# A recommender tower on one core: id comparisons without row sums, ids in three runs with gaps, fewer chunks on ScalarE

## The reference

```python
e = jnp.stack([tbl_0[ids[:, 0]], ..., tbl_25[ids[:, 25]]], axis=1)   # tables of 1000, 1250, 12500 or 125000 rows
combined = jnp.concatenate([dense_features[:, None, :], sparse_features], axis=1)
interactions = jnp.einsum('bnd,bmd->bnm', combined, combined)
interactions_flat = interactions[:, _TRIU_I, _TRIU_J]
z = jnp.concatenate([dense_features, interactions_flat], axis=1)
h = jnp.concatenate([z, r_dense_features], axis=1)
h = jnp.maximum(h @ W_top1 + b_top1, 0.0)      # (607, 512)
h = jnp.maximum(h @ W_top2 + b_top2, 0.0)      # (512, 256)
y = h @ W_top3                                 # (256, 1)
```

## Time and profile before

| | us |
|---|---|
| median of 3 runs | 109.49 |
| lowest and highest | 109.1, 110.28 |
| the profiled execution | 109.33 |
| its span in the profile | 107.4 |
| busy: TensorE, VectorE, ScalarE, GpSimd | 98.3, 86.0, 64.4, 64.5 |

### The profile page before, as it was taken

The page is one execution under the profiler, slowest core; times in us unless marked ns, Lnnn a source line. Parts: engine busy times, 40 slices in busy tenths (PEclk is TensorE's granted clock), DMA queues, the critical chain, the costliest instruction groups (busy, mean ns, idle before and its releaser), DMA issues.

```text
span 107.4 us, 3972 instructions
## 1 busy us (share of the span) xinstructions
PE 98.3 (92%) x1657; PEld 80.4 (75%) x1657; DVE 86.0 (80%) x255; ACT 64.4 (60%) x110; POOL 64.5 (60%) x68
## 2 busy tenths in 40 slices
PE   5969897997999899998999999999999997999991
PEld 2337576764766788877899887999798866998890
DVE  4799999999999999999999999999572436078121
ACT  5699989999999997809989474846300040001210
POOL 3577778777777778777777777777777700000000
PEclk9999999999999999999999999999999999999999
DMA  2999985747567847999782852112222110000000
GB/s 59 319 288 329 396 266 169 206 135 228 168 173 236 247 146 219 329 326 315 252 279 63 227 167 55 49 49 55 55 58 67 52 31 6 0 6 0 0 6 1
DMA packets 10575, 16.19 MB, mean 151 GB/s; under 512 B 2352, under 2 KB 6478, under 8 KB 10558
## 3 DMA queue, kind: packets, MB, share of 16 engines
q1 hardware_dynamic: 8398, 11.62, 34.0%
q0 software_dynamic: 2016, 4.13, 13.3%
q10 hardware_dynamic: 144, 0.19, 0.5%
HBM read 15.94 MB, written 0.00 MB: 148 GB/s over the span
## 4 chain that ended last, share of the span: by engine, by line
POOL 57%; issue 18%; PE 15%; DMA 6%; POOLq 1%; DVE 1%; DVEq 0%
POOL rows_sb L530 57%; PE h_ps L675 3%; DMA rows_sb<-in_tbl,ids_sb 3%; PE h_ps L650 3%; DMA ids_sb<-in_ids 2%; PE gram_ps L594 2%; PE h_ps L619 1%; PE turn_ps L650 1%; POOLq L293 1%; PE gram_ps L650 1%; PE turn_ps L619 1%; PE h_ps L658 1%; PE gram_ps L611 1%; PE turn_ps L594 1%; PE place_ps L611 0%
## 5 line engine op out<-in xcount | busy, mean ns | idle before, releaser
L530 POOL DMA_INDIRECT rows_sb<-in_tbl,ids_sb x63 | 63.6, 1009 | 20.9 <-issue 18.9
L571 PE MATMUL turn_ps<-onehot_sb,high_sb 128*128 128x512 f32 (+2 forms) x118 | 41.9, 367 | 3.5 <-DVE low_sb L807 1.4
L798 DVE TENSOR_SCALAR_CACHE_REDUCE onehot_sb<-lookup_ids_sb,first_sb 128x256 fp32r<-128x256 int16 (+2 forms) x79 | 43.6, 598 | 0.0
L572 PE MATMUL turn_ps<-onehot_sb,low_sb 128*128 128x512 f32 (+2 forms) x118 | 38.9, 342 | 0.0
L571 PEld LDWEIGHTS turn_ps<-onehot_sb,high_sb 128*128 128x128 f32 x118 | 22.2, 188 | 9.5 <-DVE low_sb L807 2.4
L572 PEld LDWEIGHTS turn_ps<-onehot_sb,low_sb 128*128 128x128 f32 x118 | 22.3, 189 | 1.6
L739 ACT ACTIVATE onehot_sb<-lookup_ids_sb,first_sb 128x512 fp32r<-128x512 int16 (+2 forms) x31 | 18.8, 621 | 2.3 <-PE turn_ps L572 2.2
L807 DVE TENSOR_TENSOR low_sb<-table_sb,high_sb 128x640 fp32r<-128x640 f32 (+1 forms) x26 | 19.4, 757 | 0.0
L729 ACT CAST high_sb<-table_sb 128x640 fp32r<-128x640 f32 (+1 forms) x26 | 17.0, 672 | 3.0 <-PE turn_ps L572 2.8
L594 PE MATMUL gram_ps<-feats 128*32 128x27 f32 x960 | 12.8, 196 | 1.1 <-DVE feats L701 0.4
L747 ACT ACTIVATE onehot_sb<-onehot_sb 128x768 fp32r<-128x768 f32 (+4 forms) x13 | 13.6, 1049 | 0.1
(11 more groups left out here) (53 smaller groups left out, 74.2 us busy)
## 6 DMA issues: line engine op xcount, KB each, us to landing
table_sb<-in_tbl SPq DMA_DIRECT2D x13, 256.0 KB, 3.5
table_sb<-in_tbl SPq DMA_DIRECT2D x7, 320.0 KB, 3.6
lookup_ids_sb<-in_lookup_ids SPq DMA_DIRECT2D x12, 128.0 KB, 2.4
table_sb<-in_tbl SPq DMA_DIRECT2D x6, 192.0 KB
rows_sb<-in_tbl,ids_sb POOLq DMA_INDIRECT x63, 3.3
w1p_sb<-in_w_pairs SPq DMA_DIRECT2D x1, 768.0 KB
w1d_sb<-in_w_dense SPq DMA_DIRECT2D x1, 512.0 KB, 6.3
w_sb<-in_w SPq DMA_DIRECT2D x1, 512.0 KB, 6.0
```

The lines of the kernel that those rows point to most:

```text
L530: pool.indirect_dma_start(out=rows_sb[:, GATHERS.index((tile, slot)), :], out_offset=None, in_=tables[f], in_offset=bass.IndirectOffsetOnAxis(
L571: nc.tensor.matmul(bank, high_sb[0:rows, u % 2, c, :], picked, start=c == 0, stop=False)
L572: nc.tensor.matmul(bank, low_sb[0:rows, u % 2, c, :], picked, start=False, stop=c == CHUNKS[u] - 1).then_inc(chunk_used, 1)
L798: nc.vector.tensor_scalar(onehots(u, [c])[:, 0, :], lookup_ids_at(u), row_ids_sb[:, row:row + 1], None, ALU.is_equal, ALU.add, accum_out=m ...
```

## The change

VectorE's comparison loses its second operation and its second output, and is a plain compare. The ids of a lookup, which lay in one run of 512, 384 or 256 numbers, now lie in three runs of 172, 128 or 86 with a gap of two numbers behind each, and are read as three runs; the one-hot chunk that is written is one run of 516, 384 or 258. TensorE multiplies the first 512, 384 or 256 columns of it, as before. ScalarE's distances read the three runs too.

`ACT_CHUNKS` gives ScalarE 30 chunks, where it had 33: 14 (15) in lookups 0 to 5, 7 (7) in 6 to 8, 9 (11) in 9 to 12. VectorE makes the other 88 (85). All four order tables are written anew.

```diff
+ID_RUNS = 3
+def id_columns(u):
+    return B - LOOKUP_FROM[u] * P
+def id_run(u):
+    return 2 * -(-id_columns(u) // (2 * ID_RUNS))
+ID_GAP = 2
+IDS_MAX = ID_RUNS * (id_run(0) + ID_GAP)
-ACT_CHUNKS = [2,3]*6+[3]
+ACT_CHUNKS = [3, 2, 2] * 4 + [2]
...
-    lookup 0 0:8; lookup 1 0:8; turn 0 0; lookup 2 0:7; turn 0 1; lookup 2 7; lookup 3 0:3; turn 0 2; lookup 3
+    lookup 0 0:8; lookup 1 0:4; turn 0 0; lookup 1 4:8; lookup 2 0:2; turn 0 1; lookup 2 2:8; lookup 3 0:5; turn
...
 SP_ORDER = """
-    ids; table 0; id; table 1; table 2; dn; w1d; table 3; table 4; table 5; table 6; mask; table 7; table 8;
-    table 9; w1p; table 10; sm; w2; table 11; table 12
+    ids; table 0; id; table 1; table 2; table 3; table 4; w1p; w2; table 5; dn; w1d; table 6; table 7; sm; table
+    8; mask; table 9; table 10; table 11; table 12
...
         def lookup_ids_at(u):
             ids_at = lookup_ids_sb[:, u % TABLE_BUFS, :] if u > 0 else first_ids_sb
-            return ids_at[:, LOOKUP_FROM[u] * P:B]
+            ids_at = ids_at[:, 0:ID_RUNS * (id_run(u) + ID_GAP)].rearrange("p (r c) -> p r c", r=ID_RUNS)
+            return ids_at[:, :, 0:id_run(u)]
+        def onehot_runs(u, c):
+            return onehots(u, [c])[:, 0, :].rearrange("p (r c) -> p r c", r=ID_RUNS)
...
-                picked = onehots(u, [c])[0:rows, 0, :]
+                picked = onehots(u, [c])[0:rows, 0, 0:id_columns(u)]
...
-                nc.scalar.activation(onehots(u, [c])[:, 0, :], lookup_ids_at(u),
+                nc.scalar.activation(onehot_runs(u, c), lookup_ids_at(u),
                                      ACT.Abs, bias=row_ids_sb[:, row:row + 1], scale=-1.0).then_inc(distance_made, 1)
...
-                nc.vector.tensor_scalar(onehots(u, [c])[:, 0, :], lookup_ids_at(u),
-                                        row_ids_sb[:, row:row + 1], None, ALU.is_equal, ALU.add,
-                                        accum_out=matches_sb[:, row:row + 1]).then_inc(onehot_dve, 1)
+                nc.vector.tensor_scalar(onehot_runs(u, c), lookup_ids_at(u), row_ids_sb[:, row:row + 1], None,
+                                        ALU.is_equal).then_inc(onehot_dve, 1)
```

More of the change, by code:

```diff
@@ L235 @@
+    3 1 2; layer2 2 1; dense1 3 2 3; place 3 0 16; place 3 16 32; dense1 3 3 4; bias2 3; layer1 3 0 1; layer1 3
+    1 2; layer1 3 2 3; layer1 3 3 4; layer2 3 0; layer2 3 1
 """
 ACT_ORDER = """
-    distance 0 6; cast 0 0; distance 0 7; cast 0 1; distance 1 5; cast 1 0; distance 1 6; onehot 0; distance 1
-    7; onehot 1; cast 1 1; cast 2 0; distance 2 6; copy lookup 0; cast 2 1; distance 2 7; dense; cast 3 0;
-    onehot 2; cast 3 1; distance 3 5:7; copy turn 0 0; copy lookup 1; distance 3 7; copy turn 0 1; copy lookup
@@ new lines @@
+    cast 8 0; onehot 7; twin 1; distance 8 8; copy turn 1 1; cast 8 1; distance 8 9; onehot 8; distance 9 7;
+    cast 9 0; twin 2; copy lookup 7; twin 3; cast 9 1; distance 9 8; cast 10 0; cast 10 1; distance 9 9;
+    distance 10 8; onehot 9; copy lookup 8; distance 10 9; copy turn 1 3; copy lookup 9; cast 11 0; onehot 10;
+    distance 11 8:10; onehot 11; cast 11 1; copy lookup 10; distance 12 8; cast 12 0; copy turn 2 1; place 0 0
+    32; cast 12 1; distance 12 9; onehot 12; copy lookup 11; place 1 0 32; copy lookup 12; copy turn 2 3; copy
@@ L258 @@
-    onehot 8 1:4; low 8 0; onehot 8 4; merge 0 16 32; onehot 8 5; low 8 1; onehot 8 6:8; place 0 0 32; dense;
-    copy turn 1 2; onehot 9 0:4; low 9 0; onehot 9 4:7; low 9 1; low 10 0; onehot 10 0:2; copy turn 1 4; onehot
-    10 2:4; copy turn 2 0; relu1 0 0 4; low 10 1; onehot 10 4:8; onehot 11 0:2; low 11 0; onehot 11 2:6; low 11
-    1; onehot 11 6; low 12 0; onehot 12 0:6; low 12 1; onehot 12 6; merge 1 0 16; merge 1 16 32; copy turn 2 2;
-    place 1 0 32; merge 2 0 16; layer3 0; relu1 1 0 4; merge 2 16 32; copy turn 3 0; copy turn 3 2; copy turn 3
@@ new lines @@
+    turn 1 0; onehot 7 7; onehot 8 0:3; low 8 0; onehot 8 3:6; low 8 1; onehot 8 6:8; onehot 9 0:3; low 9 0;
+    onehot 9 3:5; copy turn 1 2; onehot 9 5; low 9 1; onehot 9 6; onehot 10 0; merge 0 0 16; onehot 10 1; low 10
+    0; onehot 10 2:6; low 10 1; onehot 10 6:8; copy turn 1 4; onehot 11 0:2; low 11 0; onehot 11 2; merge 0 16
+    32; low 11 1; onehot 11 3:7; dense; onehot 11 7; onehot 12 0:3; copy turn 2 0; onehot 12 3; place 0 0 32;
+    onehot 12 4; low 12 0; onehot 12 5; low 12 1; merge 1 0 16; onehot 12 6; merge 1 16 32; onehot 12 7; relu1 0
```

69 lines of the change are left out of this document (36 added, 33 removed).

## The result

The changed kernel takes 112.25 us, median of 4 runs (111.9 to 112.29), against 109.32 (109.1 to 110.28) for the kernel before beside it: a ratio of 1.024, with an interval of 1.018 to 1.031. It is slower, by about 2.9 us, and lies outside the range that the prediction gave. The profiled execution took 112.29 us, with a span of 110.4.

What follows compares the result with a forecast made beforehand. GpSimd's gathers were taken to set the end: 107.4 us span, 0.0 from VectorE, ScalarE and SyncE, -0.1 tail, 0 +- 1.0 gathers, gives 107.3, with 1.93 around it 109.2 us; range 107.7 to 111.2.

Steps and rivals of the forecast that it cites:

- What bounds the kernel before: The end hangs on GpSimd's 63 gathers in a row; TensorE waits 0.46 us at `turn 3 4` for the last.
- The sign of being wrong that the prediction had named: Wrong if TensorE doesn't wait for the last gather, comparisons prolong gathers, or the tail differs by more than 0.5 us.
- The comparison without its sum: VectorE's plain compare takes 0.06 us less at each width; 85 comparisons give back 5.1 us.
- first rival: VectorE's comparisons run on two ports, 0.34 us each, and hold GpSimd's gathers: 111.9 us, 10%.
- The orders of TensorE, VectorE, ScalarE: Most of TensorE's 2.4 us wait for a `low` goes; it reaches the last turns 2 to 3 us sooner.
- The third rival, TensorE late: In the moved steps a turn stands before its gathers and TensorE comes late: about 110.3 us, 8%.
- Gathers: On GpSimd, 0.94 us except over a `low`, mean near 1009 ns; the new places are a random draw, 0 +- 1.0 us.
- SyncE's order: Two weights go ahead of table 5, 3.2 us of transfer, hidden; 0.0 in the sum.
- Three chunks more: One of 516 and two of 258 columns move to VectorE, costing it 1.3 us; VectorE's term in the sum stays 0.0.
- The tail: Behind `turn 3 4`, 0.1 us less, since the wait of `place` of tile 3 for a late `merge` goes.

Runs made afterwards that it cites:

- experiment 7: Kernel before, sums and single run kept, VectorE's comparisons 60 columns narrower (result not the reference's): 110.17 us, ratio 1.003.
- experiments 1: Kernel before with its order tables and ACT_CHUNKS, but ids in three runs and the plain comparison: 110.37 us, ratio 1.011.
- experiment 2: Kernel before with only the sum dropped from the comparison, ids in one run: 113.69 us, ratio 1.037.
- experiment 5: Kernel after with VectorE's comparisons 54 columns narrower, so that each costs what was forecast (result not the reference's): 109.43 us, ratio 1.000.
- experiment 6: Kernel after with the three chunks given back to ScalarE (33, as before): 111.67 us, ratio 1.021.
- experiment 4: Kernel after with SyncE's order of before alone: 111.99 us, ratio 1.026.

## Why the prediction was wrong

*What bounds the kernel before.* Half right. VectorE's pace was worth nothing in those orders (experiment 7), and in experiments 1 and 2 the end came later together with the last gather. But "whatever makes TensorE earlier only makes that wait longer" was wrong: a faster VectorE made TensorE wait in tile 0, and not at the end. The sign of being wrong that the prediction had named is there: in the kernel after the last gather is not what TensorE waits for, it had landed 2.9 us before.

*The comparison without its sum.* This step failed: "I take 0.61, 0.47 and 0.34 us ... 0.06 less than now", and with it the term of 5.1 us. Measured are 0.658, 0.520 and 0.390: 0.01 less, so that the 85 comparisons give back 0.9 us, not 5.1. The mistake was in the choice of the nearest row. The `low` of 512 columns has no sum and takes 0.60, but it is another instruction with 4-byte inputs; its 0.07 us less than the comparison were read as the price of the sum. The other bound, "nothing saved (0.67)", was the true one, and the range should have been built as if it could be. It was not: the forecast put VectorE at 3.8 us less in every case but the first rival's. It was 0.6 us more: 34 x 0.658 + 23 x 0.520 + 31 x 0.390 = 46.4 us after, 33 x 0.667 + 23 x 0.533 + 29 x 0.400 = 45.9 before, which agrees with the busy times of the page, 86.5 and 86.0. Experiment 5 shows that this one number was enough for the time: with the price as forecast the kernel takes 109.43 us, for 109.2 predicted.

*The orders of TensorE, VectorE, ScalarE.* "I expect most of that to go" was said of the wait for a `low`; it went from 2.4 to 4.6 us, and from 3.3 to 8.6 with the waits for it that the profile put down to "issue". "TensorE gets to the last turns some 2 to 3 us sooner" became 3.3 us later. Both rest on the failed step: the new orders are good only for a VectorE that is not late. The likely reason is that the new TensorE order has taken most of the work on tile 0 out from between the lookups, which was the cover for a late VectorE. At the forecast price it would not have been 2 to 3 us sooner either: in experiment 5 `turn 3 3` begins 1 us later than before, of which 0.5 is the later start of that run. So the predicted time came out there in part by luck: TensorE had about the work left that it has in the kernel before, and no gain was turned into waiting at the end. The prediction weighed what VectorE's time would bring, and never what the new orders do if it does not come. The two can be told apart now. By runs: the comparison with old orders 110.37, with new orders and the old number of chunks 111.67, with the three chunks more 112.25. The 1.1 us of the first, by its trace, is the draw of the gathers in that kernel, which the kernel after did not have, so these steps do not add up to a sum; its own loss is all TensorE's.

*The third rival, TensorE late,* is the one that came, at 8% and 110.3 us. Its mechanism was named, its route was not: not a turn that stands before its gathers, but lookups that stand before VectorE. Its price was too small since it began from a TensorE 2 to 3 us ahead.

*The first rival* did not come in this kernel, and experiment 2 shows it whole, 113.69 us for a priced 111.9: mean gather 1081 ns, the last one 4.6 us late where 2.7 was put down. Its 0.34 us a comparison used a fixed part of 0.07, which no row shows; with the 0.13 of the prediction's own rows it would have been 0.13 + 512 x 0.52 ns = 0.40, and 0.396 is what was measured. The reason given against it, three runs into one, holds.

*Gathers.* Right: comparisons hold none, gathers take 0.94 us except over a `low`, with a mean of 1004 ns; their last issue moved by 0.27 us, within 0 +- 1.0. The start of the run is 0.6 us later (first comparison at 4.03 us instead of 3.43), so without it they would have been 0.3 earlier.

*SyncE's order.* Right, no difference beyond the measurement (experiment 4).

*Three chunks more.* 1.4 us of VectorE, as forecast (1.3), and some 0.5 us of the time (experiment 6), where the sum had nothing.

*The tail.* "0.1 us less" was 0.28 less. Right in sign, no matter in size.

## What to carry to other kernels

Before an edit is priced from a neighbouring row, ask whether the two instructions differ in anything else; where the price is known only within bounds that decide the case, work the case through at each bound, orders included. An order written for one pace of an engine can cost more than it brings when that pace does not come: look at what cover it takes away from between the waits. And an engine's time is worth what the end asks of it: the same 5 us of VectorE were worth 0 in one order and some 2.7 in the other.
